# A GpSimd product ahead of a remainder, and output blocks copied out between the preceding step's scans

## What is computed

```python
ek = exp(min(k, 30));  ekv = ek * v                     # k = v = f, r = x
a = a * decay + ekv_t ;  b = b * decay + ek_t           # forward, and again in reverse
num = nf + nb - ekv + euk * v ;  den = df + db - ek + euk
y = sigmoid(r) * num / max(den, 1e-8) * gain
h = silu(y @ rw1.T + rb1);  logits = (h @ rw2.T + rb2)[:, :16] + gates
coeff = softmax of the two largest logits, else 0
out = x + y @ W.T + bias + ((y @ A.T) * coeff) @ B.T
```

## Time and profile before

| | us |
|---|---|
| median of 3 runs | 689.52 (688.38 to 690.01) |
| the profiled execution's own time | 688.6 |
| its span, first to last instruction | 686.6 |
| TensorE busy in it | 598.7 (87%) |
| VectorE busy | 526.6 (77%) |
| GpSimd busy | 368.1 (54%) |
| ScalarE busy | 357.1 (52%) |
| mean granted clock of TensorE | 0.957 of full |

### The profile page before, as it was taken

One profiled execution on the slowest core, in us unless ns is written; L12 is line 12 of the kernel. 1 busy time (PEld: TensorE's weight loads), 2 busy tenths in 40 slices (PEclk: granted clock), 3 DMA queues, 4 the chain that ended last, 5 costly groups with the idle time before them and its releaser, 6 DMA issues.

```text
span 686.6 us, 7030 instructions
## 1 busy us (share of the span) xinstructions
PE 598.7 (87%) x2626; PEld 490.1 (71%) x2626; DVE 526.6 (77%) x573; ACT 357.1 (52%) x418; POOL 368.1 (54%) x183
## 2 busy tenths in 40 slices
PE   0153588989999937999999999999999999999997
PEld 0132466768878825887888878888888888888886
DVE  7999999999999999998899797979897532021202
ACT  4777789785656666655655554656465420011000
POOL 1789997867868876647544753565465501000100
PEclk9976799989999978999999999999999999999999
DMA  5323476522945831234423360427132402040022
GB/s 190 122 90 121 124 254 205 194 100 71 215 107 121 203 113 64 74 113 160 141 73 113 109 198 32 153 63 242 33 116 84 124 29 66 27 153 1 25 67 76
DMA packets 33169, 78.42 MB, mean 114 GB/s; under 512 B 4720, under 2 KB 4848, under 8 KB 33136
## 3 DMA queue, kind: packets, MB, share of 16 engines
q1 hardware_dynamic: 30832, 73.79, 33.2%
q0 software_dynamic: 2304, 4.20, 3.8%
HBM read 57.00 MB, written 20.97 MB: 114 GB/s over the span
## 4 chain that ended last, share of the span: by engine, by line
PE 49%; DVE 25%; POOL 16%; issue 7%; ACT 1%; DMA 1%; SPq 0%; DVEq 0%; POOLq 0%; ACTq 0%
PE acc L925 15%; PE acc L927 15%; PE acc L926 15%; DVE mix L713 5%; POOL mix L602 4%; POOL kv L580 4%; POOL yr L586 4%; DVE yr L747 3%; DVE mix L708 3%; DVE eu L723 3%; DVE kv L718 2%; DVE xo L754 2%; POOL y_lo L612 2%; DVE mix L734 2%; PE acc L936 1%
## 5 line engine op out<-in xcount | busy, mean ns | idle before, releaser
L925 PE MATMUL acc<-y_hi,wa_hi 128*128 128x512 f32 x640 | 258.5, 404 | 59.7 <-POOL y_lo L612 52.7
L926 PE MATMUL acc<-y_lo,wa_hi 128*128 128x512 f32 x640 | 255.3, 399 | 0.0
L927 PE MATMUL acc<-y_hi,wa_lo 128*128 128x512 f32 x640 | 254.8, 398 | 0.0
L925 PEld LDWEIGHTS acc<-y_hi,wa_hi 128*128 128x128 f32 x640 | 124.1, 194 | 89.3 <-POOL y_lo L612 54.1
L927 PEld LDWEIGHTS acc<-y_hi,wa_lo 128*128 128x128 f32 x640 | 123.8, 194 | 26.7
L926 PEld LDWEIGHTS acc<-y_lo,wa_hi 128*128 128x128 f32 x640 | 124.2, 194 | 25.6
L602 POOL TENSOR_TENSOR mix<-mix,kv 128x1024 f32<-128x1024 f32 x31 | 74.3, 2397 | 75.7 <-DVE mix L692 59.4
L754 DVE SCALAR_TENSOR_TENSOR xo<-acc,bias_sb,xo 128x512 f32<-128x512 f32 x64 | 46.4, 735 | 75.2 <-PE acc L927 75.2
L612 POOL TENSOR_TENSOR y_lo<-yr,y_hi 128x1024 fp32r<-128x1024 f32 x31 | 74.3, 2398 | 50.2 <-ACT y_hi L402 50.2
L625 POOL TENSOR_TENSOR wx_lo<-xa,wx_hi 128x512 fp32r<-128x512 f32 x16 | 20.9, 1329 | 129.3 <-ACT wx_hi L470 129.3
L580 POOL TENSOR_TENSOR kv<-mix,kv 128x1024 f32<-128x1024 f32 (+1 forms) x32 | 75.4, 2356 | 5.3 <-DVE mix L734 5.3
(11 more groups left out here) (98 smaller groups left out, 738.3 us busy)
## 6 DMA issues: line engine op xcount, KB each, us to landing
kv<-f_cm SPq DMA_DIRECT2D x32, 512.0 KB, 3.6
yr<-x_cm SPq DMA_DIRECT2D x32, 512.0 KB, 3.4
out<-xo SPq DMA_DIRECT2D x64, 256.0 KB, 4.2
xo<-x_cm SPq DMA_DIRECT2D x64, 256.0 KB, 3.9
out<-xo POOLq DMA_DIRECT2D x16, 256.0 KB, 6.8
xa<-w_base SPq DMA_DIRECT2D x5, 512.0 KB, 3.5
xo<-w_base SPq DMA_DIRECT2D x3, 512.0 KB, 5.7
xo<-w_router_a SPq DMA_DIRECT2D x2, 480.0 KB, 3.6
```

The costliest lines, as they stand in the source:

```text
L925: nc.tensor.matmul(out_ap, wh, yh, start=start, stop=False)
L926: nc.tensor.matmul(out_ap, wh, yl, start=False, stop=False)
L927: return nc.tensor.matmul(out_ap, wl, yh, start=False, stop=stop)
```

## The change

On GpSimd in step 9, `p1(10)` now stands ahead of `split_wx(0)`. On VectorE, the blocks 3 to 6 of groups 2 to 6 are evacuated one step earlier: block 3 after the backward scan of the denominator (`AFTER_BWD_DEN`), block 4 after `p2`, block 5 after `sum_den`, block 6 after `scale_e`, all of them ahead of the backward scan of the numerator; block 7 stands in the old step after the forward scan. Group 7 keeps its places, and where neither step has scans (group 6) the sequence is the old one. SyncE's, ScalarE's and TensorE's lists are unchanged.

```diff
+        last_blocks_at = {(-1, AFTER_BWD_DEN): 3, (-1, AFTER_P2): 4, (-1, AFTER_SUM): 5, (-1, AFTER_SCALE): 6,
+                          (0, AFTER_FWD): 7}
...
-                if s in (CB + 1, CB + 4):
-                    split_wx((s - CB) // 4)
+                if s == CB + 4:
+                    split_wx(1)
                 if s + 1 < UNITS:
                     p1(s + 1)
+                if s == CB + 1:
+                    split_wx(0)
...
+            def last_blocks(s, place):
+                for late in (-1, 0):
+                    G = ends_at.get(s - late, -1)
+                    if SPLIT <= G < GROUPS - 1 and (late, place) in last_blocks_at:
+                        evacuate(G, last_blocks_at[late, place])
+
...
-                ending = ended >= 0
+                ending = ended == GROUPS - 1
                 if ending:
                     evacuate(ended, 3)
                     evacuate(ended, 4)
...
                 first_groups(s, AFTER_FWD)
+                last_blocks(s, AFTER_FWD)
...
                 first_groups(s, AFTER_BWD_DEN)
+                last_blocks(s, AFTER_BWD_DEN)
                 if s < UNITS:
                     p2(s)
                 first_groups(s, AFTER_P2)
+                last_blocks(s, AFTER_P2)
                 if s < UNITS:
                     sum_den(s)
                 first_groups(s, AFTER_SUM)
+                last_blocks(s, AFTER_SUM)
                 if s + 1 < UNITS:
                     scale_e(s + 1)
+                last_blocks(s, AFTER_SCALE)
```

More of the change, by code:

```diff
@@ L161, in base_from @@
             return HALF if G < SPLIT else 0
-        (AFTER_FWD, AFTER_FWD_NUM, AFTER_RATIO, AFTER_BWD_DEN, AFTER_P2, AFTER_SUM, AFTER_BWD_NUM) = range(7)
+        (AFTER_FWD, AFTER_FWD_NUM, AFTER_RATIO, AFTER_BWD_DEN, AFTER_P2, AFTER_SUM, AFTER_SCALE, AFTER_BWD_NUM) = range(8)
         hidden_at = {(CB, AFTER_BWD_NUM): 0, (CB + 3, AFTER_SUM): 1}
```

## The result

The changed kernel takes 699.09 us (median of 6, 697.53 to 702.63) against 689.04 us of the kernel before (6 runs): ratio 1.0152, 95% interval 1.0127 to 1.0177, 10.05 us slower. The forecast was 698.0, range 693.5 to 701.5. Differences in us are between medians; the ratios can differ from the quotient of the medians by a few units of the last digit. The profiled execution of the changed kernel is one of the slower of the six, 700.86 us with a span of 698.9; a second profiled one has 697.76 and 695.8.

What follows compares the result with a forecast made beforehand. TensorE bounds the second half; the first is a braid of the units' chain and TensorE. Part 1's 5.95 plus part 2's 2.5 (-0.87 + 1.4 + 0 + 2.0) made 8.5 us: 698.0 us forecast, range 693.5 to 701.5.

Steps and rivals of the forecast that it cites:

- Part 1: Product of unit 10 ahead of the remainder in step 9: 3.85 us of TensorE lateness plus 2.1 of low clock, 5.95.
- The handing on: VectorE's routing of group 1 waits for TensorE's logits and passes on all 3.85 us, units 14 and 15 included.
- its rival: Rival stated for `product_first`: the 8.90 us pause before unit 14 takes up TensorE's loss, shrinking to about 2.5; 689 to 690.
- The clock in step 9: Clock 0.50 behind TensorE's new pause of about 4.6 us costs 2.1 us, with ends of 0 and 3.2.
- Group 2: With block 3 evacuated earlier, TensorE's wait at the group's end goes: 0.87 us won.
- Group 3: A stall and four evacuations delay the backward scan; TensorE's wait for unit 23 grows to 2.2 us: 1.4 us lost.
- the rival with more low clock: Chance 0.15: longer low clock in step 9 (+1.1) and low clock behind the pause for unit 23 (1.6), together 700.7.
- Group 4: Same stall and scans, but the lateness ends in VectorE's wait of 2.44 us for group 5's logits: 0.
- Group 5: Last backward scan 3.44 us later; TensorE gets a new pause of 1.9 us for unit 31: 2.0 us lost.
- The stall in front of block 3: VectorE arrives before block 3 is ready at the ends of groups 3 to 5 and waits 0.6 to 0.8 us.
- the prediction's comparison of 2.29 with 2.41 us: TensorE pauses of 2.29 us left its clock at 1.00, one of 2.41 was followed by 0.50.

Runs made afterwards that it cites:

- product_first: The kernel before with only the product of unit 10 ahead of group 0's remainder on GpSimd, evacuations as before: 695.04 us against 689.02, ratio 1.0092.
- product_first_fill: The filled pause: as `product_first`, plus 12 of group 0's base matmuls ahead of TensorE's wait for the remainder: 690.99 us, ratio 1.0022 to the kernel before.
- blocks_group3: The kernel before with the evacuations moved for group 3 alone: 692.29 us, ratio 1.0055.
- blocks_only: The kernel before with only the evacuations of groups 2 to 6 moved, GpSimd's order as before: 694.32 us, ratio 1.0076.
- blocks_group2: The kernel before with the evacuations moved for group 2 alone: 688.14 us against 688.90, ratio 0.9993.
- blocks_group5: The kernel before with the evacuations moved for group 5 alone: 691.22 us, ratio 1.0034.

## Why the prediction was right, point by point

**Bound.** That the end is set by TensorE's waits and its clock held in every trace.

**Part 1, the order on GpSimd.** The remainder ended at 158.3 (forecast 158.6), and TensorE's `expert` came 3.4 to 3.6 us later (forecast 3.85). The difference is that the product began a little earlier than 153.6 and the two halves took 2.48 us; the choice of the short duration of the earlier trace rows over the 3.07 of the earlier trace rows was right. What the Trainium skill, "GPSIMD Engine Reference", section "Key points", says, that GpSimd and VectorE are in each other's way when VectorE's instruction has two SBUF inputs, agrees with this row again: beside the scan the pair took 2.48 us. It decided little, 0.5 us.

**The handing on.** As forecast: routing of group 1 with a wait of 3.90 us, units 14 and 15 behind it by the same amount, waits for unit 14 of 8.90 us in the earlier trace rows and here. `product_first` against its rival shows it by a run of its own, and the filled pause shows that it is TensorE's lateness.

**The clock in step 9.** It was low behind the pause, for longer in one trace than in the other: 6.45 - 3.57 = 2.9 and 4.96 - 3.37 = 1.6 us of cost. The forecast had 2.1 with bounds of 0 and 3.2. Part 1 alone measured 6.0, forecast 5.95. That it fits so closely is luck: the first term was 0.3 to 0.5 too large, and the second came out between 1.6 and 2.9.

**Group 2.** The wait for block 3 went. In the second trace of the changed kernel the routing of group 3 gains 4.97 - 4.07 = 0.9 us on that of group 2, forecast 0.87. In the first it loses 0.7, by the low clock at 275 us.

**Group 3.** Unit 23 came 1.45 us later in both traces (8.64 - 7.18, 5.52 - 4.07), forecast 1.4. **The term that was missing** is what follows: the routing of group 4 is later by another 1.6 us in both. The wait was 2.46 us, not 2.2, and the low clock came behind it in all four traces that have this wait. I had put that under the rival with more low clock, at a chance of 0.15, and reckoned with 2.2 us of pause. The pause came out 0.2 longer than 0.83 + 1.4 because TensorE had been held a little at the end of group 3 as well, which I had overlooked: in the trace of the kernel before, the weight load in front of the first product of group 4 waits 0.29 us for the evacuation of block 3, and the matmuls there stand 0.25 and 0.33 us apart instead of 0.23:

```profile
393.86 0.19 PEld L936 LDWEIGHTS acc<-y_hi,wr 128*128 128x128 f32 x1 [0.29 <-DVE xo L754]
```

With block 3 evacuated earlier TensorE arrives 0.17 us sooner at a unit that comes later. `blocks_group3`, which has no gain at group 2, has the same 2.46 us.

**Group 4.** Nothing, as forecast: the routing of group 5 is later by as much as that of group 4 (488.22 before, 498.44 and 495.34 after, 10.2 and 7.1).

**Group 5.** VectorE's last scan came 3.5 us later than the lateness at hand (10.2 us), behind four evacuations and a stall of 0.77 us, against 3.44 forecast. VectorE, then GpSimd, in the changed kernel, to be laid beside the earlier trace rows:

```profile
543.99 0.75 DVE L759 SCALAR_TENSOR_TENSOR xo<-acc,bias_sb,xo 128x512 f32<-128x512 f32 x1 [0.77 <-PE acc L943]
...
548.89 2.33 DVE L739 TENSOR_TENSOR_SCAN mix<-d_ps,mix 128x1023 f32<-128x1023 f32 x1
...
558.74 2.35 POOL L615 TENSOR_TENSOR y_lo<-yr,y_hi 128x1024 fp32r<-128x1024 f32 x1 [2.56 <-ACT y_hi L405]
```

TensorE got a wait of 1.78 us for it: 1.94 us lost in both traces, forecast 2.0; alone 2.3.

The stall in front of block 3 came at the ends of groups 3 to 5, 0.74, 0.97 and 0.77 us where 0.6 to 0.8 was forecast, and in the first trace at group 2 as well, 1.47 us, where TensorE was late by its clock.

**The sum.** Forecast 8.5, measured 10.05 between the medians (12.3 and 9.2 in the two traces). The low clock behind unit 23, 1.6 us in both traces, is as large as the whole difference, so that is the term that was put at nothing. The time came within 1.1 us of 698.0 partly because the forecast started from a median of 689.52, 0.5 above that of the six runs. The prediction also called the wait at the logits of group 2 one that nothing here touches; the change doesn't, but it and the clock behind it differ from execution to execution. The rest of what parts the traces is the clock in step 9 and at the logits of group 2, and the six runs spread over 5 us.

## What to carry to other kernels

A wait of one engine is slack only if what it waits for doesn't itself go through that engine: follow the awaited unit back until the two chains meet, and see who waits for whom there. Moving an engine's side work earlier moves the scans behind it later, so put it between the last input that the bounding engine waits for and the next, and look up what else is queued there (here a `silu`). Where a bounding engine pauses before a late operand, work that it has to do anyway can stand in front of the wait; here that also kept its clock at 1.00, where it had been 0.58.

## What the runs showed of the hardware

Behind TensorE's pauses of 2.45 and 2.46 us for unit 23 the clock fell to 0.50 in all four traces that have them (0.66 on average over 5 us), and behind those of 1.78 us for unit 31 it stayed at 1.00 in all four. The length of the pause alone doesn't decide: early in the kernel one of 2.33 us was followed by 0.68 over 5 us (second trace of the kernel before, at 82.46) and one of 2.36 us by 1.00 (first trace of the changed kernel, at 118.48), which also means that the prediction's comparison of 2.29 with 2.41 us was thinner evidence than it looked.

At the logits of group 2 the pause differs between executions of the same program, and it goes with the clock of the stretch before it, behind the wait for unit 15 (clocks are the mean over 5 us; the runs whose edits touch this stage are left out):

| trace | clock behind the wait for unit 15 | pause at the logits, us | clock behind it |
|---|---|---|---|
| before | 0.50 | 1.39 | 1.00 |
| before, second | 0.72 | 2.43 | 0.66 |
| changed | 0.67 | 2.18 | 0.66 |
| changed, second | 0.50 | 1.04 | 1.00 |
| `product_first` | 0.50 | 1.01 | 1.00 |
| `product_first_fill` | 0.62 | 1.96 | 0.71 |
| `blocks_only` | 0.61 | 1.91 | 0.72 |
| `blocks_group2` | 0.68 | 2.25 | 0.66 |
| `blocks_group3` | 0.60 | 1.91 | 0.72 |
| `blocks_group5` | 0.66 | 2.17 | 0.66 |

Where the clock came back within the first stretch, TensorE was through sooner, waited 1.9 us or more for VectorE's `silu`, and had a partly low clock again behind that wait; where it stayed at 0.50, the wait was 1.4 us or less and the clock behind it 1.00. So the quicker return of the clock won nothing at the logits, and the low clock behind them cost 1.6 us between the routings of groups 2 and 3 in the changed kernel (72.54 against 70.96 us). In the kernel before, the time hardly tells (688.6 and 688.57 us for the two traces), since its waits further on took the lateness up: for block 3 of group 2, 0.60 us in the one and none in the other, and for unit 23, 0.83 and 0.52. The two traces of the changed kernel still differ at the end by all that parts them there, and its six runs spread over 5 us where those of the kernel before spread over 1.6. What decides the clock behind the wait for unit 15 in an execution of the same program was not tried.
